# Feed-forwards two batches behind attention, and two of them at the front of a scan

## The reference, cut to what matters

```python
# layer 0
xn = rms_norm(x) * (1 + scale) + shift          # scale, shift from cond
o  = attention(xn @ W_qkv, 16 heads, q and k rms-normed per head)
x1 = o + o @ W_out
x  = x + relu(x1 @ w_up + b_up + lora) @ w_down + b_down + lora   # 4-bit weights, 512 -> 2048 -> 512
# layer 1
q_trace = rk4_scan(q0 = p0 = cond, drive = x, coupling)   # 256 steps, 4 evaluations a step, tanh(q) @ coupling.T
x  = x + moe(q_trace)                                     # 8 routed experts and a shared one
```

## Time and profile before

| | |
|---|---|
| median of 3 runs | 2984.52 us (2979.22 to 2985.33) |
| span of the profiled execution | 2987.5 us (its own device time is not listed apart) |
| TensorE matmul busy | 2810.5 us, 94% |
| VectorE, ScalarE, GpSimd busy | 1750.8, 1123.1, 1357.7 us |
| mean granted TensorE clock | 0.930 |
| layer 0 | to 918.4 us |
| 32 steps of the scan alone | to 1152.9 us |
| groups with expert tiles | to the end |

### The profile page before, as it was taken

The page is one execution under the profiler, slowest core; times in us unless marked ns, Lnnn a source line. Parts: engine busy times, 40 slices in busy tenths (PEclk is TensorE's granted clock), DMA queues, the critical chain, the costliest instruction groups (busy, mean ns, idle before and its releaser), DMA issues.

```text
span 2987.5 us, 132423 instructions
## 1 busy us (share of the span) xinstructions
PE 2810.5 (94%) x49096; PEld 2455.4 (82%) x49104; DVE 1750.8 (59%) x6278; ACT 1123.1 (38%) x4968; POOL 1357.7 (45%) x3466
## 2 busy tenths in 40 slices
PE   6889999989997978999999999999999999999998
PEld 4357777777776867999998999899899899899987
DVE  2646655654564445666666666666666666666654
ACT  1323433565453323333333333333333333333322
POOL 0320001111114666666665666566566566566600
PEclk8679999999995556999999999999999999999999
DMA  4712322443340001444443444444444444344376
GB/s 145 218 61 89 102 91 90 139 160 133 107 162 28 3 3 50 132 125 135 130 127 120 132 130 127 128 128 130 126 130 128 126 129 129 122 133 130 123 225 200
DMA packets 137204, 360.45 MB, mean 121 GB/s; under 512 B 15889, under 2 KB 24721, under 8 KB 136593
## 3 DMA queue, kind: packets, MB, share of 16 engines
q1 hardware_dynamic: 136336, 354.17, 38.2%
q10 hardware_dynamic: 672, 3.67, 0.3%
HBM read 323.31 MB, written 34.47 MB: 120 GB/s over the span
## 4 chain that ended last, share of the span: by engine, by line
PE 64%; DVE 2%; issue 2%; ACT 1%; DMA 0%; DVEq 0%; POOL 0%; SPq 0%; POOLq 0%
PE pscan L1312 14%; PE pscan L1308 13%; PE pg L1220 12%; PE pd L1265 11%; PE pu L1220 11%; PE pd L1238 1%; PE pu L1230 1%; PE pg L1230 1%; ACT th L1130 0%; DVE state L1440 0%; PE prouter L1327 0%; DVE carry L1440 0%; PE prouter L1335 0%; DMA wgu<-w_split 0%; DVE pscan L1426 0%
## 5 line engine op out<-in xcount | busy, mean ns | idle before, releaser
L1308 PEld LDWEIGHTS pscan<-th,carry 128*128 128x128 f16 x16384 | 561.9, 97 | 86.9 <-ACT th L1130 65.9
L1308 PE MATMUL pscan<-th,carry 128*128 128x8 f16 x16384 | 566.6, 167 | 46.2 <-ACT th L1130 46.2
L1312 PE MATMUL pscan<-th,carry 128*128 128x16 f16 x16384 | 561.9, 170 | 3.2 <-DVE th L1423 2.5
L1312 PEld LDWEIGHTS pscan<-th,carry 128*128 128x128 f16 x16384 | 486.4, 97 | 4.8 <-DVE th L1423 4.8
L1130 ACT ACTIVATE th<-state 128x32 f16<-128x32 f32 x768 | 176.2, 229 | 727.9 <-DVE state L1440 727.8
L1220 PE MATMUL pg<-qh,wgu 128*128 128x256 f16 x3168 | 428.1, 274 | 14.2 <-issue 14.1
L1265 PE MATMUL pd<-hg,wd 128*128 128x256 f16 x3168 | 429.1, 274 | 3.0 <-DMA wd<-w_split 3.0
L1220 PE MATMUL pu<-qh,wgu 128*128 128x256 f16 x3168 | 429.0, 275 | 0.0
L1440 DVE TENSOR_REDUCE state<-pscan 128x32 f32<-128x96 f32 x768 | 197.8, 257 | 276.7 <-PE pscan L1312 272.2
L1220 PEld LDWEIGHTS pg<-qh,wgu 128*128 128x128 f16 x3168 | 294.4, 98 | 52.2 <-issue 15.5
L1220 PEld LDWEIGHTS pu<-qh,wgu 128*128 128x128 f16 x3168 | 295.2, 98 | 34.8
(11 more groups left out here) (226 smaller groups left out, 4802.3 us busy)
## 6 DMA issues: line engine op xcount, KB each, us to landing
wgu<-w_split SPq DMA_DIRECT2D x264, 512.0 KB, 3.5
wd<-w_split SPq DMA_DIRECT2D x264, 384.0 KB, 3.1
parts_mem<-in_w_tiles SPq DMA_DIRECT2D x120, 256.0 KB, 3.1
w_split<-parts_mem SPq DMA_DIRECT2D x99, 256.0 KB, 2.7
late<-in_w_tiles SPq DMA_DIRECT2D x78, 256.0 KB, 3.1
w_split<-late SPq DMA_DIRECT2D x33, 128.0 KB, 3.0
out<-oo SPq DMA_DIRECT2D x8, 512.0 KB, 3.6
xs<-in_x SPq DMA_DIRECT2D x1, 3584.0 KB, 13.8
```

The lines of the kernel that those rows point to most:

```text
L1308: mm(pscan[:, 0, m * B:(m + 1) * B], clo[:, k, m * P:(m + 1) * P], th[:, k, 0, :], start=(m == 0 and k == 0), stop=False, skip_group_check ...
L1312: ins = mm(pscan[:, 0:2, m * B:(m + 1) * B], chi[:, k, m * P:(m + 1) * P], th[:, k], start=False, stop=(k == NC - 1), skip_group_check=True)
```

## The change

The feed-forward of batch n now runs beside attention of batch n + 2. Batches 0 and 1 have none beside them; those of batches 6 and 7 do their first 32 tokens at the end of layer 0 and the other 224 at the front of the scan. The scaled inputs, biases and lower-half buffers are kept for two batches, one buffer of expert parts goes (five to four). The fill is 768 products: 36 in stage 0, then nine a stage, so that stages 1 to 82 have products and 83 to 127 have none; each second fill reuses the memory of the expert tiles, so that their first loads wait for the fill's last product. Within batch 0 `restore` is split into `unpack` and `correct`, and for the first four pieces both stand ahead of VectorE's wait for the head norm.

```diff
-        part_in = [... 3 in parts_mem] + [late[:, 1152:1152 + N], late[:, 1664:1664 + N]]
+        part_in = [... 3 in parts_mem] + [late[:, 2 * NC * T:2 * NC * T + N]]
-        PARTS, DEPTH = 3 * TILES, 5
+        DEPTH = 4
...
# ScalarE
-                ffn = b > 0
+                ffn = b >= 2
...
-                    if not ffn and c:
-                        weights_high(c - 1)
+                    if not b:
+                        weights_high(c)
...
+            scaled_high(B - 1)
+            for n in (B - 2, B - 1):
+                for half in range(2):
+                    act.wait_ge(S["p_up"], first(n, half))
...
+                    if n == B - 1:
+                        act.wait_ge(S["p_dn"], 2 * (B - 2) + 1)
+                    act.activation(hid[:, half * RELUS:(half + 1) * RELUS, 0, 0:G], ...)
# TensorE
-            batch(0, False, True)
-            with pe.Fori(1, B - 1) as b:
-                batch(b, True, True)
-            batch(B - 1, True, False)
+            batch(0, False, True, 0)
+            batch(1, False, True, 1)
+            with pe.Fori(1, B // 2 - 1) as i:
+                batch(2 * i, True, True, 0)
+                batch(2 * i + 1, True, True, 1)
+            batch(B - 2, True, True, 0)
+            batch(B - 1, True, False, 1)
...
+            first_tokens_up(B - 2)
             pe.wait_ge(S["d_x1"], B)
+            pe.wait_ge(S["d_x2"], 2 * (B - 2) + 2)
+            first_tokens_up(B - 1)
+            first_tokens_down(B - 2)
+            first_tokens_down(B - 1)
# VectorE
                 for c in range(NC):
+                    if not b:
+                        unpack(c)
+                        correct(c)
                     dve.wait_ge(S["a_hr"], b * NC + c + 1)
...
-                    if not ffn:
-                        restore(c)
+                if not b:
+                    unpack(NC)
...
-                    if not ffn and h + NC < PIECES:
-                        restore(h + NC)
+                    if not b and h + NC < PIECES:
+                        correct(h + NC)
+                        if h + NC + 1 < PIECES:
+                            unpack(h + NC + 1)
# layer 1
-        FILL, PAUSE = 5, 3
+        FILL, OPENING = 9, 36
         def fill_stage(n):
-            return n // FILL + (PAUSE if n >= NC * HC * 3 else 0)
+            return 0 if n < OPENING else 1 + (n - OPENING) // FILL
...
             def group(seg, old):
                 done = seg * TILES + 2
+                if not old:
+                    sp.wait_ge(S["f_down"], 4)
                 load_up(0, 0, done)
...
-                            for n in range(2 * NC * HC * 3):
+                            for n in range(4 * PRODUCTS):
                                 if fill_stage(n) == 4 * t + s:
                                     fill(n)
```

More of the change, by code:

```diff
@@ L71, in scan_parts, with scaled_inputs @@
     return parts
+def scaled_inputs(late):
+    halves = [late[:, n * NC * T:(n + 1) * NC * T].bitcast(F16) for n in range(2)]
+    return [half.rearrange("p (c h t) -> p c h t", c=NC, h=2) for half in halves]
 def layer0(nc, dram, xs, wk, w_split, carry, ffn):
@@ L170, in layer0, with first @@
         RELUS = HC // 2
+        def first(n, half):
+            return (B - 2) * RELUS + 2 * (n - B + 2) + half + 1
         ffn_qk, ffn_last = [[], [0], [1], [2, 3, 4]], [29, 30, 31]
@@ L389, in relus @@
                         if ffn and part < HC and part % 2:
-                            relu(b - 1, part // 2)
+                            relu(b - 2, part // 2)
                 def highs(at):
@@ L531, in ffn_part, with batch @@
                         ins.then_inc(S["p_dn"], 1)
-            def batch(b, ffn, more):
+            def batch(b, ffn, more, slot):
+                opening = isinstance(b, int) and b == 0
                 pe.wait_ge(S["d_xn"], b + 1)
@@ L546, in head_norm @@
                     mm(Rb[c % 2][:], headones[:], sqh[:, c % 2].rearrange("p a t -> p (a t)"), start=True, stop=True).then_inc(S["p_hr"], 1)
-                if ffn:
+                if not opening:
                     values(lambda: None)
@@ L558, in batch @@
                         head_norm(c - 1)
-                    if not ffn:
+                    if opening:
                         lora(c)
@@ L610, in batch @@
                         if ffn:
-                            ffn_part(b - 1, part)
+                            ffn_part(b - 2, part, slot)
                     for j in range(HPC):
-                        if not ffn and HPC * c + j + NC < PIECES:
+                        if opening and HPC * c + j + NC < PIECES:
                             lora(HPC * c + j + NC)
@@ L622, in batch @@
                     for part in ffn_last:
-                        ffn_part(b - 1, part)
-                else:
+                        ffn_part(b - 2, part, slot)
+                elif opening:
                     pe.wait_ge(S["split"], PIECES)
@@ new lines, in _, with first_tokens_up @@
+            batch(1, False, True, 1)
[4 more added lines that the diff above has]
+            batch(B - 1, True, False, 1)
+            def first_tokens_up(n):
+                for m in range(HC):
+                    for k in range(NC):
+                        for w, q in ((0, 0), (0, 1), (1, 0)):
+                            ins = mm(first_up[n][m // RELUS][:, m % RELUS * G:(m % RELUS + 1) * G], w_up[:, k, w, m * P:(m + 1) * P], x1s[n % 2][:, k, q, 0:G],
+                                     start=(k == 0 and w == q), stop=(k == NC - 1 and w == 1))
+                    if m % RELUS == RELUS - 1:
+                        ins.then_inc(S["p_up"], 1)
@@ new lines, in first_tokens_down @@
+            def first_tokens_down(n):
+                for m in range(NC):
+                    for k in range(HC):
+                        if m == 0 and k % RELUS == 0:
+                            pe.wait_ge(S["d_up"], first(n, k // RELUS))
+                        for w, q in ((0, 0), (0, 1), (1, 0)):
+                            ins = mm(first_dn[n][:, m * G:(m + 1) * G], w_dn[:, k, w, m * P:(m + 1) * P], hid[:, k, q, 0:G],
+                                     start=(k == 0 and w == q), stop=(k == HC - 1 and w == 1))
+                ins.then_inc(S["p_dn"], 1)
@@ L821, in batch @@
                 if ffn:
-                    second(b - 1, 1)
+                    second(b - 2, 1)
                 if b == B - 1:
@@ L837, in lows @@
                 for part in group:
-                    if b and part < HC and part % 2:
-                        hidden_low(b - 1, part // 2)
+                    if b >= 2 and part < HC and part % 2:
+                        hidden_low(b - 2, part // 2)
             normed_input(0)
@@ L1143, in step @@
                     if not tile:
-                        for j in range(HC // 2):
+                        for j in range(2 * PAIRS):
                             if pair_stage(j) + 1 == 4 * t + s:
```

181 lines of the change are left out of this document (89 added, 92 removed).

## The result

The changed kernel takes 2956.27 us, the median of 4 runs (2952.67 to 2957.87), beside 2984.93 (2979.22 to 2985.61) for the kernel before on the same chip. The ratio is 0.9909, with a 95% interval of 0.9895 to 0.9923: faster by 28 us. The forecast was 2950, 6 us too low, inside its range of 2932 to 2978. The two profiled executions lie a little further apart, 2987.5 and 2952.9 us.

A forecast was written before the change was run, and what follows sets the result against it. TensorE was taken as the bound, with waits in layer 0 and at half its clock in the scan's first steps. Terms -27 - 6 + 1 + 5.6 + 0 - 8 = -34.4 us gave 2950 us, range 2932 to 2978.

The forecast's parts named there:

- Batch 0, -27: Batch 0 of layer 0: correcting pieces before the head norm wait removes TensorE's idle; 27 us gained, bounds -15 and -31.
- Only the first quad gains, about 2 us: Batch 0's quads: the first gains about 2 us as its unpacking precedes the scores; later ones only swap an unpacking's place.
- The third rival: Batch 0's front held by code loads or piece splitting, batch 1 hardly gaining: -15 and -2, total 2966 us; chance 0.15.
- Batch 1, -6: Batch 1 of layer 0, attention alone after losing 384 products: 6 us gained, bounds -2 and -13.
- the low end: Batch 1: gain of 4.5 us at half the clock, near 12 at full; the forecast stayed near the lower.
- Batches 2 to 7, +1: Layer 0: four expert-part buffers instead of five may make VectorE wait in batches 2 and 3; 1 us lost, 0 to +3.
- End of layer 0, +5.6: End of layer 0: doubled 128x32 products and batch 7's wait for shared hidden memory cost 5.6 us, 5 to 7.
- Between the layers, 0: Gap before layer 1: held expert loads may let it start earlier, opening products fit in; 0 us, bounds -2 and 0.
- The walk, -8: Scan's first steps up to the expert groups: filled stages of 1.66 us at full clock; 8 us gained, bounds -10 and 0.
- the 2 us kept for the first stages: Scan's start: 2 us of the saving counted off for the first stages, leaving -8 us.
- the 36 opening products are such a run: Scan's start: 36 back-to-back products raise TensorE's clock to full, like the 3.8 us run that raised it before.
- The first two rivals: In the fill, the clock stays at half (3022 us, chance 0.09) or swings between its levels (2986 us, chance 0.06).

The follow-up runs named there:

- experiment 1: Kernel before with only batch 0's reorder (VectorE unpacks and corrects a piece before waiting for the head norm): 2965.7 us beside 2985.8, ratio 0.9936.
- Experiment 2: Changed kernel with w_out and x, except batch 1's part of x, loaded behind all codes: 2950.5 us, ratio to the kernel before 0.9891.
- experiment 8: Three separate edits; the one meant here is the changed kernel with the hidden of batch 7's first tokens in columns of its own: 2955.0 us.
- experiment 3: Changed kernel without the opening block of 36 products, nine a stage from stage 0 on: 2957.3 us.
- experiment 4: Kernel before with the first 36 fill products as one block in stage 0, then five a stage as before: 2984.4 us, ratio 1.0001.
- experiment 7: Kernel before with nine products a stage instead of five in its fill of one feed-forward, no opening block: 2986.0 us, ratio 1.0007.

## Why the prediction was right, and where it wasn't

The sign held, and the sum was off by 6 us: a gain of 34.4 us was forecast and 28.7 measured by the medians. Part of that closeness is luck: the gain of batch 0 was put 10 us too high and that of batch 1 5 us too low, and they partly made up for each other. With batch 0 at its mean of -17, the stages of the table that the change touches add up to -28.

- **Batch 0, -27: about -17.** The mechanism was right, and experiment 1 shows it alone. The idle of three times 4.94 us went, and the first scores came 31.7 us after the first low-rank product (30.0 in experiment 1), 24 to 25 us less than before, near the 25.5 of the forecast. The step that failed is "Only the first quad gains, about 2 us", with the codes of piece 5 "1 or 2 us after VectorE wants them": the first quad lost 2.7 us. The later quads, put at no change, lost too: by the means of the executions all four together lost 7 us, 2.4 of them in the first, and nine of their 12 low-rank products were at half the clock instead of seven. The load of x (14.8 us) was named as what comes late next, yet only the one piece behind it was costed. Pieces 5 to 7 all stood behind x or `w_out`, with waits of 5.70, 0.98 and 2.28 us. A queue that was hidden by slack had lost the slack: the head groups had become 24 us shorter. Experiment 2 took those waits away and batch 0 became 13 us shorter, 30 less than before by the means and so all that the forecast had promised. The third rival, the loads holding batch 0, was thus half true: it held the quads, not the head groups.
- **Batch 1, -6: -11.3.** The bare quad was priced near enough: 33.4 us for the first three, 2.5 of them for the next batch's sum of squares, and 11.6, 10.5 and 9.9 measured, 32.0 in sum, the first with the burst of maxima. Wrong was the choice of the low end. The sum of its rows gave 4.5 us; from first scores to output product it measured 47.05 us for a forecast of 50.1, the output product 7.17 for 9.65, and the head groups 1.2 us less than before for no change. The output product is the part that varies: where it did take 9.0 to 9.2 us and the maxima stood as before, batch 1 took 89.0 to 89.5, still 10 us less than before.
- **Batches 2 to 7, +1: +4.4.** The term was sized for two batches. Four buffers cost 0.7 us in each of batches 2 and 3 and about 1 in 4 to 7; some 2.5 us more, which lie at the later stores, were not foreseen and are not explained.
- **End of layer 0, +5.6: +5.1**, by the chain that was written down; the hidden kept apart (experiment 8) takes 2.2 of it back.
- **Between the layers, 0: -1.3**, inside its bounds, from the held loads, as was named.
- **The walk, -8: -8.0.** The stage is 1.66 us as worked out. But the 2 us kept for the first stages went elsewhere: the clock was at 1.00 from stage 1 on, and five stages were lengthened to 1.84 to 2.55 us. And the reason given for the clock, "the 36 opening products are such a run", is not what decides: the block raises it, but without it the clock rises by stage 3 all the same (experiment 3), and with it but five a stage it falls before stage 2 and does not come back (experiment 4). What decides whether it rises is how many products a stage has: begun at half the clock, nine raise it, in the old fill too (experiment 7), and five do not. The first two rivals, the clock staying down or swinging in the fill, fall: 1.00 from 904 to 1042 us.
- The Trainium skill (TensorE: Matmul & The Clock Gate, A second HAM failure mode: psum-queue depth-cycling) tells of a kernel in which short idles between groups of products make the clock swing. Here the fill with six a stage was idle 9 of 160 us in pieces of 0.1 us or so a stage and held 1.00, so in this kernel the trace doesn't agree; the two stages lost at 904.7 us in one profile, after an idle of 2.04 us, are the nearest thing to it.

## What to carry to other kernels

When a stage is made shorter, go through every load that shares a queue with what it consumes, and add up all those behind a large one, not only the first. Filler work beside a latency-bound loop may be worth more than its own time: here it holds TensorE's clock up, so that the loop with it (1.65 us) is shorter than without (1.71), and six a stage did better than nine. How thin it may be spread is to be measured: five were not enough to raise the clock. And give such filler its helpers early enough: at nine products a stage in the old fill, waits for lower halves gave back 3 us and more of what the clock had brought.

## What the runs showed of the hardware

The granted clock under the scan was at one of its two levels for whole stretches: 0.50 (1.2 GHz) with the five products a stage of before, but for the first 1 us of them where a block had raised it, and 1.00 (2.4 GHz) with six, seven or nine behind such a block, but for two stages in each of the two profiles whose idle behind the block was 2.0 us. Nine raised it without a block, within three stages; six and seven were not run without one. A bare stage took 1.64 us at the full clock and 1.71 at half, so at five a stage (1.79) the loss was not the scan's own products but the filler in front of them.

GpSimd's first instruction of layer 1 came 8.4 to 8.7 us after layer 0's last where SyncE started four expert loads at that time, and 7.0 to 8.0 where it held them.
